# An attention and feed-forward layer on one core: output projection in four column parts, another order of the first products, and more half groups in the first two steps

## What is computed

```
Q = X @ Wq + bq;  K = X @ Wk + bk;  V = X @ Wv + bv
scores = einsum('bhqd,bhkd->bhqk', q, k) / sqrt(16)
attn = softmax(scores);  out = einsum('bhqk,bhkd->bhqd', attn, v)
out = out.transpose(0, 3, 2, 1).reshape(b, s, 256)
x = layernorm(x + out @ Wo + bo)
gate = silu((x @ w_gate) * s_gate);  up = (x @ w_up) * s_up
x = layernorm(x + ((gate * up) @ w_down) * s_down)
```

## Time and profile before

| | |
|---|---|
| median of 3 runs | 600.42 us (600.18 to 600.59) |
| the profiled execution | 600.33 us, of which the profile's span is 598.6 us |
| PE busy | 588.2 us, 98% of the span |
| ACT busy | 506.6 us, 85% |
| DVE busy | 442.4 us, 74% |
| POOL busy | 54.4 us, 9% |
| mean granted clock of TensorE | 0.997 of full |

### The profile page before, as it was taken

How to read it: one execution, slowest core, us unless ns; L and a number is a source line. 1 busy time by engine, 2 the same in 40 slices (tenths; PEclk the granted TensorE clock), 3 DMA queues, 4 the chain that set the end, 5 groups by cost and what they waited for, 6 DMA issues and landing times.

```text
span 598.6 us, 10544 instructions
## 1 busy us (share of the span) xinstructions
PE 588.2 (98%) x3952; PEld 249.7 (42%) x3952; DVE 442.4 (74%) x812; ACT 506.6 (85%) x614; POOL 54.4 (9%) x51
## 2 busy tenths in 40 slices
PE   8999999999999999999999999999999999999995
PEld 7884222222222223223232322222323227988974
DVE  6673766989888767687676668888767696776876
ACT  4539999999999999999999999999999995253352
POOL 6606000000000000000000000003000001102021
PEclk9999999999999999999999999999999999999998
DMA  9466938112303020111211010112010000101102
GB/s 207 72 105 85 122 62 105 26 29 35 85 11 70 8 34 8 31 16 25 61 17 27 11 29 11 30 34 44 8 33 7 7 4 9 39 1 35 36 2 71
DMA packets 36185, 24.71 MB, mean 41 GB/s; under 512 B 24930, under 2 KB 30946, under 8 KB 35538
## 3 DMA queue, kind: packets, MB, share of 16 engines
q1 hardware_dynamic: 34740, 23.29, 23.1%
q10 hardware_dynamic: 1392, 0.72, 0.5%
HBM read 6.56 MB, written 4.33 MB: 18 GB/s over the span
## 4 chain that ended last, share of the span: by engine, by line
PE 96%; DVE 2%; ACT 1%; issue 0%; DMA 0%; SPq 0%; POOL 0%; POOLq 0%; ACTq 0%
PE ps L1254 42%; PE ps L1226 29%; PE ps L1363 10%; PE ps L1096 6%; PE ps L1340 4%; PE ps L1276 3%; PE ps L1067 1%; DVE attn_q L820 1%; PE ps L1294 1%; PE ps L1082 1%; ACT probs L654 0%; DMA out<-out_tmp 0%; SPq L511 0%; DVE xt_lo L722 0%; PE ps L1128 0%
## 5 line engine op out<-in xcount | busy, mean ns | idle before, releaser
L654 ACT ACTIVATE probs<-ps 128x1024 f32<-128x1024 f32 (+1 forms) x512 | 444.1, 1098 | 14.8 <-PE ps L1226 14.4
L1254 PE MATMUL ps<-probs,v_all 128*17 128x512 f32 x1916 | 269.0, 598 | 1.2 <-DVE attn_q L820 0.5
L1226 PE MATMUL ps<-q_slot,k_stack 51*128 51x512 f32 x1024 | 198.0, 458 | 0.0
L1226 PEld LDWEIGHTS ps<-q_slot,k_stack 51*128 51x128 f32 x1024 | 85.0, 184 | 220.1 <-ACT probs L654 206.1
L884 DVE TENSOR_SCALAR bits<-ps 128x512 int32<-128x512 f32 x66 | 45.5, 689 | 50.2 <-PE ps L1226 41.3
L1254 PE MATMUL ps<-poly,v_all 128*17 128x512 f32 x132 | 68.2, 599 | 0.0
L673 ACT ACTIVATE sg<-ps,sgate_c 128x512 f32<-128x512 f32 x32 | 22.0, 689 | 49.5 <-PE ps L1363 49.5
L1254 PEld LDWEIGHTS ps<-probs,v_all 128*17 128x17 f32 x1916 | 33.5, 95 | 61.2 <-issue 50.6
L908 DVE SCALAR_TENSOR_TENSOR poly<-poly,bits 128x512 f32<-128x512 f32 x66 | 47.2, 715 | 7.2 <-DVE poly L904 0.5
L904 DVE SCALAR_TENSOR_TENSOR poly<-poly,mant 128x512 f32<-128x512 f32 x66 | 45.7, 692 | 2.3
L895 DVE SCALAR_TENSOR_TENSOR poly<-mant 128x512 f32<-128x512 f32 x66 | 45.2, 684 | 0.0
(11 more groups left out here) (99 smaller groups left out, 452.9 us busy)
## 6 DMA issues: line engine op xcount, KB each, us to landing
q_slot<-qy SPq DMA_DIRECT2D x64, 64.0 KB
k_stack<-k_part SPq DMA_DIRECT2D x12, 256.0 KB
at_dram<-attn_q SPq DMA_DIRECT2D x64, 34.0 KB
at<-at_dram SPq DMA_DIRECT2D x8, 272.0 KB, 3.0
q_slot<-qy SPq DMA_DIRECT2D x64, 32.0 KB
x_tok<-in_L_attn_X SPq DMA_DIRECT2D x14, 128.0 KB, 5.9
k_stack<-k_part SPq DMA_DIRECT2D x12, 128.0 KB
out<-out_tmp SPq DMA_DIRECT2D x12, 128.0 KB, 2.2
```

The lines of the kernel that those rows point to most:

```text
L654: nc.scalar.activation(probs[:, slot_of(g), first:2, :].rearrange("p a b -> p (a b)"), ps[:, 2 * ring + first:2 * ring + 2, :].rearrange(" ...
L1226: last = nc.tensor.matmul(ps[:, 2 * ring + half, :], k_stack[s % QUADS][base:base + ROWS, p, kt * P:(kt + 1) * P], q_slot[slot][base:base ...
L1254: last = nc.tensor.matmul(ps[32 * hh:32 * hh + VW, ACC, :], v_all[:, tiles[hh], NQ * (s % QUADS) + hh, :], prob, start=(kt == 0), stop=(kt ...
```

## The change

```
-        probs = place("probs", [P, HALVES, 2, CW], f32, at)
+        probs = place("probs", [P, HALVES + 1, 2, CW], f32, at)
...
         def poly_tiles(s):
-            return [6, 10, 13] if s == 0 else [2, 6, 10, 13] if s == 1 else [2, 5, 8, 11, 14] if s in (2, 3, 4) else [2, 6, 10, 13]
+            return [2, 5, 8, 11, 14] if s <= QUADS else [2, 6, 10, 13]
...
         def slot_of(g):
-            return (0, 2, 4, 1, 3, 5)[g % HALVES]
+            return HALVES if g == HALVES // 2 else (0, 2, 4, 1, 3, 5)[g % HALVES]
...
                 act.wait_ge(scores_ready, g + 1)
-                if g == 3:
+                if g == 4:
                     act.wait_ge(v_psum, TT // 2)
...
                 half = j % 2
+                dst = ps[:, out_bank(c, j // 2), half * HID:(half + 1) * HID]
                 for ko in range(KO):
-                    last = nc.tensor.matmul(ps[:, out_bank(c, j // 2), half * HID:(half + 1) * HID],
-                                            at32[:, ko, CH * j:CH * (j + 1), :].rearrange("p d u -> p (d u)"),
-                                            wo[:, ko, :], start=(ko == 0), stop=(ko == KO - 1))
+                    if c < LAST:
+                        for d in range(CH):
+                            last = nc.tensor.matmul(dst[UW * d:UW * (d + 1), :], at32[:, ko, CH * j + d, :],
+                                                    wo[:, ko, :], start=(ko == 0), stop=(ko == KO - 1))
+                    else:
+                        last = nc.tensor.matmul(dst, at32[:, ko, CH * j:CH * (j + 1), :].rearrange("p d u -> p (d u)"),
+                                                wo[:, ko, :], start=(ko == 0), stop=(ko == KO - 1))
...
             for u in range(UNITS):
                 scores(2 * u)
-                if u == 0:
-                    project_v(V_LATE)
                 scores(2 * u + 1)
-                if u == 1:
-                    project_v(V_LATE + 1)
+                if u < 2:
+                    project_v(V_LATE + u)
```

## The result

The changed kernel takes 605.7 us, median of 4 runs (604.99 to 606.26), against 600.5 for the kernel before (600.18 to 600.59). The ratio is 1.0087, 95% interval 1.0075 to 1.0100: slower by 0.9%. The profiled execution took 605.44 us.

The account below looks back on a forecast made before the run. TensorE was busy 98% of the span; ACT's exponentials paced whole groups, TensorE the pace without such waits. Terms 6.9 - 0.3 + 2.3 + 0 - 2.2 = +6.7 us on 600.33 gave 607.0, range 604.4 to 609.3.

Parts of the forecast that it names:

- The hole: Step 0: group 7's scores wait for DVE's first polynomial read, held by GpSimd's additions; TensorE idles from about 50.3 to 57.6.
- The twelve units behind it: Step 0, units 4 to 15 at 1.70 us each: step 1 starts at 79.5 instead of 72.53, +6.9 us.
- The clock: TensorE's granted clock falls in step 0's long wait; about 5.4 us of work at low clock cost +2.3 us.
- the sum's factor, 1 - 1.64 / 2.9: Share of low-clock time lost in step 0: a unit takes 2.9 us instead of 1.64.
- The sign "unit starts 2.5 to 3.3 us apart": Expected in the changed profile: this unit spacing in windows from about 54 to 63, with granted clock below 1.00.
- The rival in which it doesn't fall: Granted clock stays up through TensorE's wait in step 0: 604.7 us, chance 0.06.
- Steps 1 and 2: Step 1, with five half groups instead of four, takes 27.2 to 27.4 us, not 27.63: -0.3 us.
- The order of the first products: Part (b), loop start: ACT gains about 0.9 us but idles later: 0 us; without the hole, up to 0.9.
- The projection: Part (a), output projection in four column parts: 0.88 us a call instead of 1.06, twelve calls, -2.2 us.
- the sign for it: Expected in the changed profile: scores 0.88 us after the output projection's start, where they came 1.06 after.
- The rival on the other side: Step 0: GpSimd's additions end 7.2 us sooner, so the stall doesn't come: 596.6 us, chance 0.04.
- the rival that it was taken from: Output projection gains nothing, as narrow weight loads aren't hidden behind 0.22 us streams: 609.2 us, chance 0.06.

Follow-up runs that it names:

- the run with the clock held up: Changed kernel plus 60 unused identity transposes on TensorE between the scores of groups 6 and 7: 603.68 us, ratio 1.0051 to the kernel before.
- the tiles alone: Kernel before with only the five half groups in steps 0 and 1, old output projection and old order of first products: 608.03 us, ratio 1.0124.
- the fastest kernel: Changed kernel with GpSimd's additions started behind last polynomials of steps 0 to 4 and three polynomials of step 5, DVE's wait at step 6: 596.09 us.

## Why the prediction was right, point by point

Forecast 607.0 us, measured 605.7. The mechanism was the right one; several terms were mis-sized, nearly all of them towards too slow.

**The hole.** Said: DVE's first read comes at 56.82 whatever group it is for, and TensorE waits 7.3 us. Measured: read at 56.31, wait 7.08. Of the 0.5 us, 0.4 is GpSimd's start, and 0.1 the length of its additions. The start differs between executions of the same GpSimd program (46.22 to 46.91 in those whose loop starts at about the same time). That the additions are the cause was shown by leaving half of them out (5.05 us less hole for 4.9 less of additions) and by starting them elsewhere (no hole).

**The twelve units behind it** were said to take 1.70 us each. In the run with the clock held up, the way from the start of group 7's scores to step 1 is 21.4 us, where the sum had 57.62 to 79.5, 21.9: behind the hole ACT is ahead, and most units run at TensorE's own 1.65.

**The clock.** It fell, as forecast. Said 2.3 us, measured 1.7. The rate was right and the duration wrong. I had taken the 5.4 us of the program's start for the time of low clock, although no window there shows it (the granted clock stands at 1.00 in all of them). Here it was low for 3.9 us of work, and 3.9 times the sum's factor, 1 - 1.64 / 2.9, is the 1.7; in the tiles alone 6.6 us of work give 2.9, as measured. So the duration differs between executions, and the forecast's 2.3 lies between the two that were profiled. The sign "unit starts 2.5 to 3.3 us apart" failed for the same reason: the units from unit 4 on start 2.21 and then 1.66 apart in the changed kernel, since the clock was back within unit 4; the whole unit at low clock, 2.99, is in the other run. The rival in which it doesn't fall is weaker still than it was made: the clock also fell right behind a hole of 1.8 us (six additions moved ahead).

**Steps 1 and 2.** Said -0.3; measured -0.43 in step 1 and -0.20 in step 2, which before was longer than steps 3 and 4 with the same half groups. I had looked at step 1 only.

**The order of the first products.** Said: nothing with the hole, up to 0.9 us without. With the hole it was nothing (the tiles alone, 608.03, less 2.3 is the changed kernel). Without a hole it depends on what sets the pace: 0.8 us between the medians with the old tiles, nothing with the new ones.

**The projection.** Said -2.2; measured -2.3 alone and -2.5 by the steps' lengths. The narrow groups repeat at the rate that the norms' row promised: sixteen pairs pass in 0.97 us (204.37 to 205.34), 61 ns each, as in the earlier trace rows. The Trainium skill's rate of about 81 ns a pair with 128 columns, from "TensorE: Matmul & The Clock Gate", section "Back-to-back issue gap", isn't seen. But the sign for it was placed wrongly: the scores come 0.97 us after the projection's start, not 0.88. I had put the whole saving into the projection, and 0.11 of the 0.20 lies in the products ahead of it.

Added up between the profiled executions: step 1 starts 7.7 us later (predicted 9.2), steps 1 and 2 give back 0.6, the projection 2.5, which makes +4.6. The span has grown by 5.1. The other 0.5 us lies behind the loop, in a part that the change doesn't touch. That part takes 102.9 us in the profiled execution before and 103.4 in the changed kernel; in the other kernels' profiled executions it takes 102.8 to 103.4, so this may be mere spread. It is luck for the forecast, because it hides 0.5 of the 2.1 us by which the other terms came out too high.

**The rival on the other side** was put too simply. It needed the additions to end 7.2 us sooner, which is right, and its price was right too: 596.6 us without the stall, where the fastest kernel took 596.1. But it suggests that DVE need only not wait for them, and that isn't so: taking the wait away gave back 1.5 us of 8.9, because the additions themselves slow DVE.

**The range.** Its upper end, 609.3, stands 0.1 above the rival that it was taken from, 609.2; nothing hangs on it.

## What to carry to other kernels

A wait whose engine is idle anyway can still be the thing that a later edit runs into. Before work is moved ahead in an engine's program, look at what its first instruction of that kind waits for, and when that comes, not only at how much the engine has free. And before such a wait is removed, ask what it keeps apart. Here the cure was to move the work of the other engine into a gap in which DVE was waiting for TensorE, which made a kernel of 596.1 us out of one of 605.7.

## What the runs showed of the hardware that I had not expected

- DVE instructions of 128 x 512 that read and write SBUF took 1.4 to 1.8 us in place of 0.43 and 0.68 while GpSimd added in SBUF. One that read PSUM took 0.68, as without them. GpSimd's addition went from 1.25 to 1.42 us.
- GpSimd started nothing for 5.7 us between elementwise additions and a reduction over the partitions (one profiled execution), and for 6.9 to 7.7 from the end of the reduction's row to the next addition (ten of them).
- The granted clock went from full to half 0.3 us behind the end of a TensorE hole of 1.8 us in one profiled execution, and stayed at full through a hole of 2.0 us in one of another kernel. What decides this isn't settled here. It may be what split that other kernel's executions into 598.2 to 598.9 and 599.7 to 600.3 us.
- Behind holes of 7.1 and 6.8 us TensorE worked at the low clock for 3.9 us in one execution and for 6.6 in another, which cost 1.7 and 2.9 us.
- Sixteen float32 matmuls of 256 columns on four 32-column parts cost 0.86 us over a plain unit behind others of that layout, four of 256 columns on the whole array 1.06.
